# State-space scan with four steps of 32 prepared by GpSimd, attention heads issued in an order that depends on the slot, and graph scatters moved ahead of a gather

## What is computed

```python
# state-space block, per layer and direction (forward and reversed tokens)
delta = softplus(dbc[:, :32] @ dtp_w.T + dtp_b)        # (B, L, d), L = 1024, d = 64
dA  = exp(delta[..., None] * A)                        # 16 states n
dBu = delta[..., None] * Bm[:, :, None, :] * x[..., None]
h = dA_t * h + dBu_t ;  y_t = sum_n h[..., n] * C_t[n] # scan over the L tokens
out = x1 * z + x2 * z + skip

# graph attention of the expert block, 16384 nodes cut to the 8192 tokens here, 262144 edges
e = leaky_relu(a_src[src] + a_dst[dst]); alpha = softmax of e over the edges of one dst
agg = segment_sum(h[src] * alpha, dst)
```

## Time and profile before

| what | value |
|---|---|
| median of 3 runs | 11360.51 us (11357.73 to 11375.49) |
| profiled execution, its own time | 11365.2 us |
| its span, first to last instruction | 11363.4 us |
| granted TensorE clock, mean | 0.818 of full |
| state-space stage, first to last instruction of its DVE list | 621 to 6033 us |
| attention stage, slots | 6645 to 7475 us |
| graph stage, first block | 7552 to 7680 us |

### The profile page before, as it was taken

The page is one execution under the profiler, slowest core; times in us unless marked ns, Lnnn a source line. Parts: engine busy times, 40 slices in busy tenths (PEclk is TensorE's granted clock), DMA queues, the critical chain, the costliest instruction groups (busy, mean ns, idle before and its releaser), DMA issues. The chain is left out here.

```text
span 11363.4 us, 84355 instructions
## 1 busy us (share of the span) xinstructions
PE 6743.2 (59%) x21767; PEld 2848.2 (25%) x21767; DVE 7343.2 (65%) x5616; ACT 4840.1 (43%) x5351; POOL 7216.4 (64%) x4635
## 2 busy tenths in 40 slices
PE   0178888888888888888887879930000000000569
PEld 0133333333333333333333323310000000000432
DVE  8779999999999999999994357731111111112334
ACT  0066666666666666666662346621111111110123
POOL 0078888888888888888885320027777777775037
PEclk9599999999999999999998879965555555555569
DMA  0145555555555555555552000012222222220022
GB/s 9 26 137 154 155 156 153 156 154 155 154 156 153 156 153 157 155 155 157 153 155 59 1 10 1 1 5 40 18 18 18 18 18 18 18 18 8 3 55 89
DMA packets 388257, 959.57 MB, mean 84 GB/s; under 512 B 124306, under 2 KB 159762, under 8 KB 385762
## 3 DMA queue, kind: packets, MB, share of 16 engines
q1 hardware_dynamic: 303106, 930.62, 29.1%
q0 software_dynamic: 75808, 26.27, 5.3%
q10 hardware_dynamic: 9216, 1.05, 0.1%
HBM read 905.27 MB, written 50.92 MB: 84 GB/s over the span
## 5 line engine op out<-in xcount | busy, mean ns | idle before, releaser
L502 POOL TENSOR_TENSOR hC<-h,Cb 128x1024 f32<-128x1024 f32 x1536 | 3609.7, 2358 | 935.9 <-DVE h L581 934.3
L581 DVE TENSOR_TENSOR_SCAN h<-dA,B_ps 128x1024 f32<-128x1024 f32 x1536 | 3512.4, 2287 | 68.1
L285 PE MATMUL y_ps<-hC,con 128*128 128x512 f32 x6144 | 2908.9, 595 | 92.5 <-DVE gz L587 56.9
L432 ACT ACTIVATE dA<-delta,negA 128x1024 f32<-128x1024 f32 x1536 | 1762.8, 1148 | 1836.8 <-DVE h L581 1836.2
L2529 POOL DMA_INDIRECT g_got<-scratch_node,g_idx x2048 | 1946.1, 950 | 614.4 <-issue 614.4
L573 DVE TENSOR_TENSOR B_ps<-dx,B_ps 128x1024 f32<-128x1024 f32 x1536 | 1856.3, 1209 | 91.9 <-PE B_ps L279 91.9
L2545 PE MATMUL g_ps_y<-g_wout,g_hid 128*128 128x64 f32 x512 | 125.8, 428 | 2250.1 <-ACT g_hid L2585 2250.1
L285 PEld LDWEIGHTS y_ps<-hC,con 128*128 128x128 f32 x6144 | 1136.7, 189 | 1126.4 <-issue 739.5
L279 PE MATMUL B_ps<-Bpart,sel 96*128 96x512 bf16 x3072 | 925.2, 383 | 677.1 <-DVE h L581 676.0
L2615 DVE TENSOR_TENSOR g_e<-g_tgt,g_got 128x128 f32<-128x128 f32 x64 | 27.0, 422 | 1763.6 <-DMA g_got<-scratch_node,g_idx 1763.6
L2569 ACT ACTIVATE g_w_ps<-g_w 128x128 f32<-128x128 f32 x64 | 18.0, 281 | 1942.7 <-DVE g_r L2630 1942.7
(11 more groups left out here) (472 smaller groups left out, 10024.9 us busy)
## 6 DMA issues: line engine op xcount, KB each, us to landing
Cb<-scratch_c_rows SPq DMA_DIRECT2D x3072, 256.0 KB, 3.9
g_got<-scratch_node,g_idx POOLq DMA_INDIRECT x2048
eb_share<-scratch_gate_rows SPq DMA_DIRECT2D x128, 256.0 KB, 3.4
scratch_edge<-g_out SPq DMA_DIRECT2D x64, 384.0 KB, 2.4
par<-in_ssm SPq DMA_DIRECT2D x48, 395.5 KB, 5.0
...
```

What stands on the lines that cost most here:

```text
L285: last = nc.tensor.matmul(y_ps[:, hs], con[:, K_ID:K_ID + P], hC[k % DEEP][:, hs], start=(k == 0), stop=(k == STEPS - 1))
L432: A(dA[k % DEEP][:, :], delta[d][:, :], ACT.Exp, scale=negA[:, n:n + 1]).then_inc(decay_ready, 1)
L502: G.tensor_tensor(hC[k % DEEP][:, :], hst[k % DEEP][:, :], Cb[k % DEEP][:, :], ALU.mult).then_inc(prod_ready, 1)
L581: V.tensor_tensor_scan(hst[k % DEEP][:, ::step], dA[k % DEEP][:, ::step], B_ps[k % 2][:, ::step], 0.0, ALU.mult, ALU.add).then_inc(scanned, 1)
```

## The change

**State-space.** At the four steps 5, 13, 21 and 29 (`ASIDE`) the input of the scan is made in another way. ACT stores all of B and C to memory (`BCrow`, 64 rows where `Crow` had 32); SP spreads the B row of the step over `dA[k % 4]` (`fetch_aside`, two transfers, four steps ahead, behind scan k-4); POOL multiplies it with `dx` in place, three steps ahead (`input_aside`, behind the output part of step k-3). ACT writes the decay of the step to PSUM `B_ps[k % 2]`, one step ahead (`decay_aside`). The scan then reads its decay from PSUM and its input from SBUF. PE's `copies` and DVE's `input_part` of the step are gone. Semaphores count the 28 other steps of a turn and the four apart (`inside`, `aside`).

**Attention.** In a slot that follows maxima of a block 0 to 7, head 1 comes before head 0, on PE and on ACT.

**Graph.** The 64 scatters wait for `adst` alone (`link` 2) and stand ahead of the wait for the stored rows and of the gather of `ad0`.

```diff
+    ASIDE = (5, 13, 21, 29)
+    def inside(step):
+        turn, k = step
+        return turn * (STEPS - len(ASIDE)) + k - sum(m < k for m in ASIDE)
+    def aside(turn, k):
+        return turn * len(ASIDE) + sum(m < k for m in ASIDE)
...
-        Crow = some("Crow", [2 * NST, L])
+        BCrow = some("BCrow", [4 * NST, L])
...
+                def fetch_aside(k):
+                    d, n = dir_of(k)
                     for i in range(2):
                         row = c_rows[d, i * NST + n:i * NST + n + 1, :].broadcast_to([C, L])
-                        sp.dma_start(Cb[k % DEEP][i * C:(i + 1) * C, :], row).then_inc(c_here[k % DEEP], 16)
+                        sp.dma_start(dA[k % DEEP][i * C:(i + 1) * C, :], row).then_inc(aside_here, 16)
...
                         if k == 27 and not last_turn:
                             store_rows(0, t + 1)
+                        if k + DEEP in ASIDE:
+                            sp.wait_ge(scanned, t * STEPS + k + 1)
+                            fetch_aside(k + DEEP)
...
-                    if not (last_turn and k >= STEPS - 1):
+                    if not (last_turn and k >= STEPS - 1) and k + 1 not in ASIDE:
...
-                    done(A(Crow[d][:, :], pp[96:P, :], ACT.Copy))
+                    done(A(BCrow[d][:, :], pp[C:P, :], ACT.Copy))
...
+                def decay_aside(k):
+                    d, n = dir_of(k)
+                    A(B_ps[k % 2][:, :], delta[d][:, :], ACT.Exp, scale=negA[:, n:n + 1]).then_inc(aside_decay, 1)
...
+                        if ahead % STEPS not in ASIDE:
+                            act.wait_ge(scanned, s)
+                            decay(ahead)
+                    if k + 1 in ASIDE:
                         act.wait_ge(scanned, s)
-                        decay(ahead)
+                        decay_aside(k + 1)
...
+                def input_aside(t, k):
+                    own(f"dx{dir_of(k)[0]}", t)
+                    pool.wait_ge(aside_here, aside(t, k) * 32 + 32)
+                    G.tensor_tensor(dA[k % DEEP][:, :], dx[dir_of(k)[0]][:, :], dA[k % DEEP][:, :], ALU.mult).then_inc(aside_dbu, 1)
...
                     output_part(k, it * STEPS + j, first=j < SHIFT)
+                    if k + 3 in ASIDE:
+                        input_aside(t, k + 3)
...
-                def scan(k, s, first=False):
+                def scan(t, k, s, first=False):
                     step = (1, -1)[dir_of(k)[0]]
-                    dve.wait_ge(dbu_ready, s + 1)
-                    dve.wait_ge(decay_ready, s + 1)
+                    decayed, driven = dA[k % DEEP], B_ps[k % 2]
+                    if k in ASIDE:
+                        decayed, driven = driven, decayed
+                        dve.wait_ge(aside_dbu, aside(t, k) + 1)
+                        dve.wait_ge(aside_decay, aside(t, k) + 1)
+                    else:
+                        dve.wait_ge(dbu_ready, inside((t, k)) + 1)
+                        dve.wait_ge(decay_ready, inside((t, k)) + 1)
                     if not first:
                         dve.wait_ge(prod_ready, s - DEEP + 1)
...
+    def order(g):
+        block = maxima_at(g - 1)
+        return (1, 0) if block and block[1] < PER else (0, 1)
...
-                    for h in range(2):
+                    for h in order(g):
                         if g:
-                            pe.wait_ge(exped, 2 * (g - 1) + h + 1)
+                            pe.wait_ge(exped, 2 * (g - 1) + order(g - 1).index(h) + 1)
...
-                    for h in range(2):
-                        act.wait_ge(scored, 2 * g + h + 1)
+                    for n, h in enumerate(order(g)):
+                        act.wait_ge(scored, 2 * g + n + 1)
...
-                    pool.wait_ge(rows_out, 32)
-
-                    nc.gpsimd.indirect_dma_start(out=ad0[:, :], out_offset=None, in_=target_tbl,
-                                                 in_offset=Off(ap=t0[:, 0:1], axis=0),
-                                                 bounds_check=NODES - 1, oob_is_err=False).then_inc(spread, 16)
                     pool.wait_ge(places_filled, 64)
+                    pool.wait_ge(link, 2)
                     for i in range(TILES):
...
+                    pool.wait_ge(rows_out, 32)
+                    nc.gpsimd.indirect_dma_start(out=ad0[:, :], out_offset=None, in_=target_tbl,
```

41 lines of the change are left out of this document (24 added, 17 removed).

## The result

The changed kernel takes **11608.9 us** (median of 4 runs, 11601.7 to 11623.7) where the kernel before takes 11368.0 us: a ratio of 1.0213, 95% interval 1.0195 to 1.0231. It is slower by 2.1%, and the prediction, 11442 us with 11350 to 11515, had the direction but not the size. The profiled execution has a span of 11601.5 us (before 11363.4).

The account below looks back on a forecast made before the run. DVE was taken to bound the state-space stage, nearly half of the time. From 11365.2 us, state-space +136, attention -22 and graph -32 gave 11447 for the profiled execution, 11442 us as median; range 11350 to 11515.

Parts of the forecast that it names:

- What bounds the stage: State-space stage: DVE is its bound, its scans, input parts and closing product filling the list almost without idle time.
- DVE's own work, -2.8: State-space turn: four input parts save 4.96 us, register instructions waiting ahead of 24 more scans cost 2.16; net -2.8.
- Step 11, +1.0: State-space: POOL's product for step 5 delays PE's copies for step 11, so DVE waits 1.0 us a turn.
- Step 13, +3.1: State-space: B row lands late behind store and `par`, POOL stands 5 us, scan 13 waits 3.1 us (1.9 to 4.4).
- Behind step 13, +0.6: State-space: POOL's backlog delays PE's projection and copies that DVE needs at step 17; some 0.6 us a turn, an estimate.
- Step 23, grows by 1.1: State-space: DVE arrives 1.2 us earlier, PE's product of `u0` comes no sooner; the 0.57 us wait grows about 1.1.
- Step 31, 0: State-space: no added wait was forecast here; step 29, moved aside, was to keep its gain.
- Attention -22, graph -32: Attention: new head order shortens slots, -22 us (-35 to -5). Graph: scatters start earlier, -32 us (-35 to -28).
- The transfers' jam: Rival, state-space: B rows land 8.5 us or later, or steps 21 and 29 are late too; 11536 us, chance 0.10.
- registers that cost nothing: Rival, state-space: register instructions ahead of scans cost nothing, about 1.1 us a turn left; 11390 us, chance 0.12.
- the B row in time: Rival, state-space step 13: row lands before POOL asks, terms of steps 13 and 17 go; 11268 us, chance 0.10.
- the full gain: Rival, state-space: all that is taken off DVE comes through, 238 us; 11068 us, chance 0.04.

Follow-up runs that it names:

- Undoing the order in the queue: Changed kernel, but SP issues the B row of step 13 ahead of the store and `par`: 11459.1 us, ratio 1.0068.
- With PE filled: Changed kernel, plus products by a zero matrix while PE would idle, 16 in position 13 and 10 in position 21: 11533.8 us, ratio 1.0137.
- all mended: Changed kernel, B row of step 13 first, old product wait at the input part, zero products in positions 13, 21, 28, 29: 11307.3 us, ratio 0.9939.

## Why the prediction was right and wrong

The step that failed is the price of PE's work behind a wait. The sum knew that DVE would wait for PE's copies, but it let PE's own products take as long as before. They took up to twice as long, because PE's granted clock fell while PE waited for POOL. The sum had nothing for this, at steps 15, 23 and 31 alike.

- **What bounds the stage.** Right for before. After the change DVE bounds the turn only in stretches, and PE behind POOL bounds the rest; the prediction knew this for steps 11, 13 and 23 and sized it too small.
- **DVE's own work, -2.8.** A turn without its waits is 119.12 - 9.98 = 109.1 us; before 112.55 - 0.95 = 111.6: -2.5. The pieces are right: 1.33 in all steps, 2.20 from scan to scan, 2271 ns with decay in PSUM. The missing 0.3 is a matter of counting: an input part or scan that doesn't wait starts 2.20 us after a scan of 2.29, so each of the four new waits costs 0.09 more than its idle time. The waiting register at 0.09 was shown in the kernel before itself.
- **Step 11, +1.0.** 0.73 where it occurs, 0.64 in the mean, and 0.11 at step 8.
- **Step 13, +3.1.** 3.0 measured; the wait of POOL 4.76 for 5, the landing 6.9 for 7.2. Undoing the order in the queue took most of it away (0.43 left).
- **Behind step 13, +0.6.** It is 1.65, at step 15 and not 17. The step named a backlog of POOL. What the trace has there is PE, idle for 4.34 us and then at half clock. With PE filled the wait at step 15 is gone and 0.66 at step 17 is left. So the mechanism that I named is worth about the 0.6 that I gave it, and the one that I missed 0.9 more.
- **Step 23, grows by 1.1.** It grew from 0.95 to 3.23. In the two turns that I compare, 0.57 and 3.81 and so the two ends of what occurs, it divides like this. Counted from scan 20, `u0` came 0.4 us later (its POOL product for step 21 waited 0.45 for a row, for which I had taken 0) and DVE 1.2 us earlier, as forecast; but from the start of PE's product to the input part it is 4.14 us instead of 2.46. That is 1.7 us of clock. Over all turns the filling took 1.25 away.
- **Step 31, 0.** It is 1.34 in the mean, by a little the largest error of a single term. In the turn shown four matmuls take 3.53 us behind a PE that waited for POOL, and with PE filled in positions 28 and 29 the wait is 0.05. "Step 29 keeps its gain" is what failed here.
- **The sum.** Waits grew by 9.0 us a turn (0.95 to 9.98) where 5.8 were forecast. The turn missed the forecast by 6.57 - 3.0 = 3.6 us; filling PE in only two places took 2.3 off the turn.
- **The sign that I passed over.** I took 0.57 us for the wait at step 23 from one turn. The group in the earlier trace rows has 91.9 us; without the 46.1 of the stage's first wait 45.8 are left for 47 turns, 0.97 each. That doesn't agree with 0.57, and the turns of 113.7 us among those of 112.3 would have led to PE's slow product, in the trace of before.
- **Attention -22, graph -32.** -24.3 and -30.8. For the graph the term is right. For attention the sum is, and its parts are not: slots behind sums gained 0.7 and not 0.6, those without sums nothing and not 0.2, and the change of order, where it lengthens a slot, cost the 0.9 forecast.
- **The rivals.** The transfers' jam has fallen, though its 11536 us is the nearest number, and so have registers that cost nothing, the B row in time and the full gain. The range ended at 11515 because no case had a price on PE's side: every wait was counted as long as before, once it began.

What stays open: why PE's clock falls in every fourth turn of before and not in the others, at the same idle time; why the wait for the input part costs 0.09 us on a register instruction and 0.06 on a semaphore instruction; and what the 5.7 us of waits in the kernel with all mended owe to each of POOL's products.
